# A decoder layer's attention phase regrouped from steps of four heads to double-steps of eight

## The reference

```python
x = layernorm(x + self_attention(x))          # 16 heads of 64, causal mask, no biases
x = layernorm(x + cross_attention(x, ctx))    # 16 heads of 16, a mask and biases per projection
x = layernorm(x + moe(x))                     # two groups of 32 experts, top 2 of each, SwiGLU, hidden 128
```

## Time and profile before

| | before |
|---|---|
| median of three runs | 4757.99 us |
| profiled execution, its own time | 4757.9 us |
| its span | 4756.2 us |
| TensorE busy (matmuls) | 4648.3 us, 98% |
| VectorE busy | 3782.9 us, 80% |
| ScalarE busy | 3412.8 us, 72% |
| GpSimd busy | 2692.6 us, 57% |

### The profile page before, as it was taken

How to read it: one execution, slowest core, us unless ns; L and a number is a source line. 1 busy time by engine, 2 the same in 40 slices (tenths; PEclk the granted TensorE clock), 3 DMA queues, 4 the chain that set the end, 5 groups by cost and what they waited for, 6 DMA issues and landing times. The chain is left out here.

```text
span 4756.2 us, 133366 instructions
## 1 busy us (share of the span) xinstructions
PE 4648.3 (98%) x38848; PEld 3981.4 (84%) x38848; DVE 3782.9 (80%) x18827; ACT 3412.8 (72%) x13381; POOL 2692.6 (57%) x3748
## 2 busy tenths in 40 slices
PE   8999999999999999999999999999998699999998
PEld 7888888888888888888888888888887577878786
DVE  5888888888888888888888888888888356657888
ACT  5888887888888878878888878878877344444443
POOL 3455555555555555555555555555555455556777
PEclk9999999999999999999999999999999799999999
DMA  4221111211111211111111112111114499998998
GB/s 143 70 65 63 59 59 59 66 63 62 59 59 59 69 63 61 59 59 62 65 63 60 59 59 66 64 63 59 59 57 138 134 303 348 323 305 257 307 313 282
DMA packets 477441, 552.31 MB, mean 116 GB/s; under 512 B 55632, under 2 KB 408144, under 8 KB 476240
## 3 DMA queue, kind: packets, MB, share of 16 engines
q1 hardware_dynamic: 350800, 296.21, 19.8%
q0 software_dynamic: 52224, 146.87, 8.3%
q10 hardware_dynamic: 73728, 100.70, 6.9%
HBM read 266.21 MB, written 277.35 MB: 114 GB/s over the span
## 5 line engine op out<-in xcount | busy, mean ns | idle before, releaser
L534 POOL TENSOR_TENSOR yTl<-yT,yTh 128x256 fp32r<-128x256 f32 x512 | 382.7, 748 | 907.8 <-DVE yTh L991 904.7
L761 ACT ACTIVATE prob<-prob,negmax 128x128 f32<-128x128 f32 x2048 | 799.0, 396 | 103.6 <-DVE negmax L839 99.2
L761 ACT ACTIVATE xprob<-xprob,xnegmax 128x128 f32<-128x128 f32 x2048 | 792.5, 391 | 1.3 <-DVE xnegmax L839 1.3
L1165 POOL DMA_INDIRECT y_d<-y,to x576 | 564.4, 980 | 363.8 <-DVE y L1307 279.1
L1218 PE MATMUL bank<-moe,xgT 128*128 x2304 | 597.3, 382 | 4.4 <-issue 4.2
L593 POOL DMA_INDIRECT xs_d<-xrow,place x512 | 516.0, 1008 | 127.9 <-issue 127.6
L839 DVE CUSTOM_DVE_ANT_0 prob<-bank,causal 128x128 f32<-128x128 f32 x2048 | 471.5, 286 | 33.9 <-PE bank L699 20.5
L779 ACT COPY probT<-bank 128x512 f32<-128x512 f32 x512 | 300.6, 587 | 254.2 <-PE bank L709 185.1
L839 DVE CUSTOM_DVE_ANT_0 xprob<-bank,xmask 128x128 f32<-128x128 f32 x2048 | 470.5, 286 | 1.1 <-remote 1.1
L849 DVE TENSOR_TENSOR prob<-prob,inv 128x512 f32<-128x512 f32 x512 | 440.1, 860 | 20.2
L1218 PEld LDWEIGHTS bank<-moe,xgT 128*128 128x128 f32 x2304 | 394.4, 191 | 38.8 <-issue 8.5
(11 more groups left out here) (178 smaller groups left out, 14223.0 us busy)
## 6 DMA issues: line engine op xcount, KB each, us to landing
xg<-xs_d SPq DMA_DIRECT2D x576, 129.0 KB
xs_d<-blank SPq DMA_DIRECT2D x248, 272.0 KB
rows<-y_d ACTq DMA_DIRECT2D x256, 256.0 KB
xT_s<-xT SPq DMA_DIRECT2D x128, 128.0 KB
x<-x SPq DMA_DIRECT2D x128, 128.0 KB, 2.0
cT<-cT SPq DMA_DIRECT2D x128, 128.0 KB
x_d<-x SPq DMA_DIRECT2D x128, 128.0 KB, 2.0
sums<-x_d ACTq DMA_DIRECT2D x128, 128.0 KB
```

Of the source, the lines that this page charges most:

```text
L534: nc.gpsimd.tensor_tensor(yT_p[1][:, c, :], yT[:, c, :], yT_p[0][:, c, :].bitcast(F32), ALU.subtract).then_inc(y_split, 1)
L761: last = nc.scalar.activation(dst[:, h, :], dst[:, h, :], ACT.Exp, bias=src_bias[:, h:h + 1], scale=-1.0, accum_out=acc[:, h:h + 1])
L1165: nc.gpsimd.indirect_dma_start(y_d[:, :], bass.IndirectOffsetOnAxis(ap=to[:, m % NTO:m % NTO + 1].bitcast(U32), axis=0), y_s[q][:, :], Non ...
```

## The change: double-steps of eight heads

GH is 8 and a batch is two double-steps: even ones with heads 0 to 7, odd ones with heads 8 to 15. `steps_of` runs each engine's `double_step(n)` for n from -4 to 2 NB + 13; a job of batch b is due at n = 2b + AFTER[name]. Cross attention runs CROSS = 5 double-steps behind self attention. Four banks hold scores: two for self, two for cross; the transposes go into the same banks once the scores have been read out, a half ("side") of four heads each. The cross mix takes a turn in the three job banks (`xy`). ScalarE moves all q/k results, GpSimd makes both halves of y, the two norms have root instructions and semaphores of their own. `prob` of both parities is one tensor, which also serves as the staging room for weights; x and mask have one tile each.

```diff
-GH = 4
-NG = H // GH
+GH = 8
+PH = GH // 2
-JOBS = [
-    (0, "qk0", -2, 0), (0, "qk1", -2, 0), (0, "xk", 1, 0),
-    (1, "o2", 3, 0), (1, "rank", 4, D), (1, "o1", 1, 0),
-    (2, "qk2", -2, 0), (2, "qk3", -2, 0), (2, "v0", -1, 0),
-    (3, "x1t", 1, 0), (3, "x2t", 3, D), (3, "v1", -1, 0), (3, "xq", 1, 0), (3, "route", 3, D), (3, "xv", 1, 0),
-]
+EVEN = ("qk0", "o2", "qk1", "x1t", "v1", "xq", "xv", "rank", "xy")
+ODD = ("qk2", "x2t", "qk3", "o1", "route", "xk", "v0", "xy")
+AFTER = dict(qk0=-4, qk1=-4, qk2=-3, qk3=-3, v0=-1, v1=0, o1=3, xk=3, x1t=4, xq=4, xv=4, o2=8, x2t=9, route=9, rank=10)
+CROSS = 5
...
+                    def turn(n, side):
+
+                        if not live(n - 1):
+                            return
+                        pe.wait_ge(normed, 2 * (n - 1) + side + 1)
+                        if live(n):
+                            pe.wait_ge(maxed, 2 * n + side + 1)
+                        else:
+                            wait(pe, probT_in, 2 * (n - 2) + side + 1)
+                        for i in range(PH):
+                            last = nc.tensor.transpose(SELF_BANKS[side][:, i * P:(i + 1) * P], prob[:, (n - 1) % 2, side * PH + i, :], ident[:, :])
+                        last.then_inc(turned, 1)
...
+                        if live(n):
+                            score(n)
+                        if live(n - CROSS):
+                            cross_score(n - CROSS)
+                        if n % 2 == 0:
+                            job(n, "qk0")
+                            job(n, "o2")
+                            turn(n, 0)
+                            turn(n, 1)
+                            job(n, "qk1")
+                            job(n, "x1t")
+                            cross_turn(n, 0)
+                            cross_turn(n, 1)
+                            job(n, "v1")
+                            job(n, "xq")
+                            job(n, "xv")
+                            job(n, "rank")
+                        else:
+                            job(n, "qk2")
+                            job(n, "x2t")
+                            turn(n, 0)
+                            turn(n, 1)
+                            job(n, "qk3")
+                            job(n, "o1")
+                            cross_turn(n, 0)
+                            cross_turn(n, 1)
+                            job(n, "route")
+                            job(n, "xk")
+                            job(n, "v0")
+                        mix(n)
+                        cross_mix(n)
```

ScalarE's list of a double-step, and GpSimd's (each entry only where a batch is due):

```diff
+                    def double_step(n):
+                        move_y(n)
+                        exponentials(n, 0)
+                        move_qk(n, "qk2" if n % 2 else "qk0")
+                        exponentials(n, 1)
+                        move_turned(n, 0)
+                        move_turned(n, 1)
+                        move_qk(n, "qk3" if n % 2 else "qk1")
+                        cross_exponentials(n, 0)
+                        move_cross_turned(n, 0)
+                        move_cross_turned(n, 1)
+                        if n % 2 == 0:
+                            move_v(n, "v1")
+                        else:
+                            move_xk(n)
+                            move_v(n, "v0")
+                        cross_exponentials(n, 1)
...
+                    def double_step(n):
+                        if live(n - 2):
+                            split_y(n - 2)
...
+                            spread_keys(b)
...
+                            open_blocks(b)
...
+                            scatter(b, (0, 1))
...
+                            x_low(split_pair(n))
...
+                            root(1, b)
...
+                            scatter(b, (2, 3))
...
+                            nc.gpsimd.tensor_tensor(x1b[b % 2][:, :], x1[b % 2][:, :], xbo_s[:, :], ALU.add).then_inc(x1b_ready, 1)
...
+                            token_rows(b)
...
+                            root(0, b)
...
+                    def split_y(m):
+
+                        b, g = heads_of(m)
+                        c = slice(g * PH, (g + 1) * PH)
+                        pool.wait_ge(yT_in, m + 1)
+                        if g == 0:
+                            wait(pool, made["o1"], b)
+                        nc.gpsimd.tensor_copy(yT_p[0][:, c, :], yT[:, :, :]).then_inc(y_high, 1)
+                        pool.wait_ge(y_high, m + 1)
+                        nc.gpsimd.tensor_tensor(yT_p[1][:, c, :], yT[:, :, :], yT_p[0][:, c, :].bitcast(F32), ALU.subtract).then_inc(y_split, 1)
```

VectorE's two lists (the bodies of xq, xmask, xv and of the x1 and x2 instructions cut):

```diff
+                    def even_step(n):
+                        place_tokens(n)
+                        masked(n)
+                        cross_masked(n)
...
+                            steps2 = residual(n, "o2", 1, norm2_step, sum2, x1b[b2 % 2], x1b_ready, b2 + 1)
+                        normalise(n, 0)
...
+                            variance(steps2, 1)
+                        weigh(n)
+                        normalise(n, 1)
...
+                            dve.wait_ge(rsqrt_ready[1], b2 + 1)
...
+                            nc.vector.tensor_scalar(x2[b2 % 2][:, :], sum2[:, :], mv[:, 1, 0:1], rs[:, 1:2],
+                                                    ALU.subtract, ALU.mult).then_inc(x2_ready, 1)
+                        move_transposed(n, "x1t")
+                        cross_normalise(n, 0)
...
+                        cross_normalise(n, 1)
+
+                    def odd_step(n):
+                        rank_moves(n)
+                        masked(n)
+                        cross_masked(n)
+                        normalise(n, 0)
+                        move_transposed(n, "x2t")
...
+                            x_split_high(split_pair(n))
+                        normalise(n, 1)
+                        cross_normalise(n, 0)
...
+                            steps1 = residual(n, "o1", 0, norm1_step, sum1, x_s, x_in, (b1 + 1) * 16)
+                        top_two(n)
...
+                            variance(steps1, 0)
+                        cross_normalise(n, 1)
...
+                            nc.vector.tensor_scalar(x1[b1 % 2][:, :], sum1[:, :], mv[:, 0, 0:1], rs[:, 0:1],
+                                                    ALU.subtract, ALU.mult).then_inc(x1_ready, 1)
```

More of the change, by code:

```diff
@@ L394, in weight_low, with split_pair @@
                 tensor_tensor(low, staging(n), high.bitcast(F32), ALU.subtract).then_inc(LOW_DONE[n][0], 1)
-            def taken(s):
-                return (0, s - 2) if s >= 2 else (1, NG - 2 + s)
+            def split_pair(n):
+                pair, rest = divmod(n + 5, 4)
+                return pair if not rest and 1 <= pair < NB // 2 else None
             with nc.Block() as block:
@@ L427, in _ @@
                     stage(3, wo)
[L429 to L451, removed]
@@ L591, in scatter @@
                             pool.wait_ge(cleared, CLEAR * clears_for(b))
[L592 removed]
+                        for j in slots:
                             nc.gpsimd.indirect_dma_start(
@@ new lines, in mix @@
+                    def mix(n):
+                        if not live(n - 1):
+                            return
+                        b, g = heads_of(n - 1)
+                        pe.wait_ge(probT_in, 2 * n)
+                        wait(pe, yT_in, n - 1)
+                        if g == 0:
+                            pe.wait_ge(moved["v0"], b + 1)
+                            pe.wait_ge(moved["v1"], b + 1)
+                        for pair in range(PH):
+                            for side in (0, 1):
+                                f = (g * GH + 2 * pair + side) * DH
+                                last = nc.tensor.matmul(PV[HALVES[side], pair * P:(pair + 1) * P], v_s[b % 2][:, f:f + DH],
+                                                        probT[:, side * PH + pair, :], start=True, stop=True)
+                        last.then_inc(mixed, 1)
@@ new lines, in move_transposed, with residual @@
+                    def move_transposed(n, name):
+                        b = job_of(n, name)
+                        if b is not None:
+                            dve.wait_ge(made[name], b + 1)
+                            dst = x1T if name == "x1t" else x2T
+                            nc.vector.tensor_copy(dst[:, :, :].rearrange("p k t -> p (k t)"), jb(n, name)[:, 0:D]).then_inc(moved[name], 1)
+                    def residual(n, name, w, step, total_s, other, ready, count):
+                        b = job_of(n, name)
+                        steps = Steps(dve, step, 2, b)
+                        dve.wait_ge(made[name], b + 1)
+                        dve.wait_ge(ready, count)
+                        nc.vector.tensor_tensor(total_s[:, :], jb(n, name)[:, 0:D], other[:, :], ALU.add).then_inc(moved[name], 1)
+                        dve.wait_ge(moved[name], b + 1)
+                        steps.done(nc.vector.bn_stats(stats[:, w, :], total_s[:, :]))
+                        return steps
```

749 lines of the change are left out of this document (364 added, 385 removed).

## The result

The changed kernel takes 5190.1 us (median of four runs) against 4759.4 for the kernel before beside it: ratio 1.091, 95% interval [1.0885, 1.0938]. I forecast 4776 and a range of 4710 to 4840. The sign was right, the size wrong by a factor of more than 20: +431 us against the +18 of the forecast.

The account below looks back on a forecast made before the run. PE, busy for all of the attention phase, was taken as the bound. On 4757.9 us, -121 (fewer tile changes) + 163 (wait at xq) - 24 (start and tail) = +18 gave 4776 us, range 4710 to 4840.

Parts of the forecast that it names:

- PE with half as many tile changes: PE's attention phase: two groups a batch instead of four save 0.98 us, 28.49 to 27.51 us, -121 us in all.
- rival 4: PE's excesses at six places a step might belong to semaphores, not tile changes; halving groups halves them anyway; no chance given.
- One wait, at xq: PE waits for VectorE's x1T copy once a batch, in the even step: 12.3 - 10.96 = 1.3 us.
- PE's own way of 10.96 us: PE's work from v0 made to where it wants xq: 10.96 us if nothing waits.
- the chain of 12.0 without GpSimd: From v0 made through ScalarE and VectorE's queue to x1T and PE resuming: 12.0 us; 12.3 with GpSimd's contention.
- GpSimd beside VectorE: Contention in the chain to x1T: up to 0.25 us for each of three normalises, 0.1 for place_tokens; 0.3 taken.
- an exclusive lock for a whole instruction: A normalise could lose all of GpSimd's 1.29 us subtraction: +1 us a batch, +123 us; chance 0.03, within rival 2's 0.16.
- No other wait: Scores, masks, exponentials, transposes and moves of v1 and q/k all meet PE in time; only xq waits.
- Rival 2: GpSimd's root comes late for x2, ahead of x1T: each 0.5 us +0.5 a batch, about 4840 us; chance 0.16.
- Start and tail: Both ends of the attention phase gain from light double-steps: -10 us at the start, -14 in the tail, together -24.

Follow-up runs that it names:

- e6: e4 with GpSimd's wide operations (y's split, keys, x1b, token rows) one column wide from batch 2, values stale: 4613.1 us, ratio 0.971.
- e1: Changed kernel with GpSimd's wide operations (y's split, keys, x1b, token rows) one column wide from batch 2, values stale: 4751.8 us, ratio 0.999.
- e3b: Changed kernel with place_tokens moved behind the masks, x1T's copy left where it was: 5144.0 us, ratio 1.082.
- e5 split small: Changed kernel with only y's cast and subtraction and the spreading of the keys one column wide from batch 2, values stale: 5018.8 us, ratio 1.057.
- e2: Changed kernel with VectorE's x1T copy moved right behind the variance, ahead of weigh, second self normalise and x2: 4919.9 us, ratio 1.034.
- e9: e1 plus one VectorE sum ahead of the x1T copy, making PE's wait longer; GpSimd's wide operations stay small: 5121.9 us, ratio 1.078.
- e4: e3 with GpSimd's root of the second variance issued ahead of the first two scatters: 4662.3 us, ratio 0.982.
- e3: Changed kernel with both moves, x1T's copy right behind the variance and place_tokens behind the masks: 4842.8 us, ratio 1.018.
- e8: Changed kernel with place_tokens behind the masks and the root ahead of the scatters, x1T's copy still last: 4795.0 us, ratio 1.008.
- e5 rows small: Changed kernel with only x1b and the token rows one column wide from batch 2, values stale: 4948.1 us, ratio 1.042.

## Why the prediction was wrong, step by step

- *PE with half as many tile changes, 27.51 us a batch*: right. The floor is 27.49 (e6), and in the changed kernel the first three groups of an even step take 0.93, 0.97 and 0.99 us from start to start (2003.55, 2004.48, 2005.45, 2006.44) for my 0.92, 0.98 and 1.00. No run tells whether the excess belongs to the tile changes or to the semaphores that stand at the same places (rival 4).
- *One wait, at xq, released by the x1T copy*: right in place, and the formula too. PE's own way of 10.96 us and the chain of 12.0 without GpSimd give 28.55; e1 has 28.51.
- *"GpSimd beside VectorE", 0.3 us in the sum*: this is the step that failed. It measured 14.82 - 11.96 = 2.86 us. By the timeline x1 takes 0.3 more than priced, place_tokens and weigh take 2.15 + 1.38 = 3.53 us for 1.55, and normalise 1 with its reciprocal 1.51 for 0.82. That is 3.0 in all, about 0.1 of which other steps give back. I had bounded the term by the earlier trace rows, the mean of the self normalise (0.86 against 0.69), as if a collision cost a fraction of an instruction. A mean over 512 instructions says how often they met GpSimd, not what one meeting costs. And I gave only 0.1 to the short ones, although a copy of four numbers a partition lost 1.09 us there (1252 ns for 161), more than the 0.70 of the normalise.
- The Trainium skill, "SBUF — State Buffer", section SBUF: two separate sides, had it: an exclusive lock for a whole instruction. The trace agrees (1252 ns for 161, both in the groups above). I had worked out its price for one normalise alone, +1 us and +123 us of time, and given it 0.03. On the five instructions that it really meets, it is 2.86 x 123.5 = +353 us.
- *No other wait*: wrong as a consequence. place_tokens stands ahead of the masks, so its 1.4 us come back at the self transposes (0.37 us, 241 times; no such wait in e1, e3b and e5 split small). They lie within the chain and cost nothing beside it until x1T is moved (e2).
- *The clock*: not in the prediction at all. Of the loss of 3.50 us a batch 2.88 are the lock's (31.39 - 28.51) and 0.61 the drops' (32.00 - 31.39). e9 shows that the waits bring them without GpSimd's wide operations.
- *Rival 2, GpSimd late*: not so. Its root waits 1.36 us for VectorE's variance in the changed kernel. It became true in e3b, where VectorE, no longer held up in place_tokens, waits 0.5 us for the root in nearly every batch.
- *Start and tail, -24 us*: less, as far as the runs can tell. e6 is 17 us below what the middle alone gives (4751 - 121 = 4630), the changed kernel's ends give about 9.

Open: e6 is still 49 us under e4, 0.27 us a batch of it in the period (27.76 against 27.49). The waits view shows nothing there, since it leaves out gaps below 0.15 us. By the starts of PE's records 0.15 of the 0.27 lies in the odd step's self transposes: the fifth starts 0.23 us behind the fourth, where 0.11 is the rule, as it needs masks that follow VectorE's line 1078, a scan between SBUF tiles that takes 0.86 us beside GpSimd's subtraction for 0.30. So this part too is the lock, by my reading. The rest is not traced.

## What to carry to other kernels

Before a queue of VectorE is put on a critical path, lay GpSimd's timeline beside it: a copy, a TENSOR_SCALAR or an instruction with two inputs between SBUF tiles can cost VectorE the rest of GpSimd's instruction, however small it is. So short bookkeeping of this kind is placed where GpSimd has scatters or nothing, and what stands beside GpSimd's wide operations is work that reads PSUM. Price a collision by the longest case in the trace, not by a mean. Where GpSimd arrives is part of this: a move that makes VectorE earlier can slide the next instruction under the lock (x2 in e3b and e3). And look at the granted clock wherever TensorE waits again and again: here each drop cost 1.65 us on top of the wait.

## What the runs showed that I had not expected

- Not every instruction is locked. Masks (scores from PSUM) take 0.28 us beside GpSimd's products, where a copy of 128x4 in SBUF takes 1.25 us beside its subtraction. A reciprocal between SBUF tiles is not held up either: 93 times in e3 between 600 and 3400 us it starts within GpSimd's subtraction and takes at most 0.17 us, while the product behind it waits for the subtraction's end:

```profile
2026.67 1.27 POOL L571 TENSOR_TENSOR yTl<-yT,yTh 128x512 fp32r<-128x512 f32 x1
2026.92 0.16 DVE L1036 RECIPROCAL xinv<-xtotal 128x4 f32<-128x4 f32 x1
2027.12 1.37 DVE L1038 TENSOR_TENSOR xprob<-xprob,xinv 128x512 f32<-128x512 f32 x1
```

- Scatters (1.0 us each on GpSimd) held up neither x2 nor a normalise: x2 beside one takes 0.41 (e8), beside the token rows 1.79 (e3).
- The granted clock of a stretch with a wait of TensorE in each batch: 1.00 with 1.1 us (e8) and 1.3 us (e5 rows small), 0.97 with 2.0 (e5 split small), 0.98 with 2.6 (changed kernel), 0.96 with 2.7 (e9), 0.97 with 3.1 (e3b). It doesn't follow the wait's length alone; why is open.
